# The second softmax exponential of 392 columns in three tiles of each image as a polynomial on VectorE, and a TensorE order planned with a look ahead

## What is computed

```python
g = clip(bn(conv1x1(l)), 0, 6)                       # values, 64 channels
theta = l[:, :32]
f = einsum('niab,nicd->nabcd', theta, theta)         # scores, 3136 x 3136 for each image
f = softmax(f.reshape(n, h * w, h, w), axis=1)       # over the queries
f = softmax(f.reshape(n, h * w, h * w), axis=2)      # over the keys
out = einsum('nabcd,nicd->niab', f, g)
out = bn(depthwise3x3(out / h * w))
return out + l
```

## Time and profile before

| | us |
|---|---|
| median of 3 runs | 5280.22 |
| lowest, highest | 5277.17, 5281.35 |
| the profiled execution | 5281.39 |
| its span, first to last instruction | 5279.5 |

### The profile page before, as it was taken

One profiled execution on the slowest core, in us unless ns is written; L12 is line 12 of the kernel. 1 busy time (PEld: TensorE's weight loads), 2 busy tenths in 40 slices (PEclk: granted clock), 3 DMA queues, 4 the chain that ended last, 5 costly groups with the idle time before them and its releaser, 6 DMA issues. The chain is left out here.

```text
span 5279.5 us, 89479 instructions
## 1 busy us (share of the span) xinstructions
PE 5199.9 (98%) x32626; PEld 2546.9 (48%) x32626; DVE 4437.3 (84%) x8974; ACT 5099.2 (97%) x3028; POOL 4447.5 (84%) x1857
## 2 busy tenths in 40 slices
PE   8999989999999999999999999999999999999997
PEld 3444444454445454545454444545454544454543
DVE  8888887888888888888888888888888888888887
ACT  7888889999999999999999999999999999999996
POOL 6666655898888998888999898899889899888897
PEclk9999989999999999999999999999999999999999
DMA  7888851222223222222221222232232322222221
GB/s 148 166 181 169 164 111 34 52 59 55 56 59 63 63 63 62 63 62 58 60 58 44 60 61 58 60 64 58 48 63 63 63 63 63 62 63 61 47 44 30
DMA packets 227138, 379.94 MB, mean 72 GB/s; under 512 B 158165, under 2 KB 175374, under 8 KB 216590
## 3 DMA queue, kind: packets, MB, share of 16 engines
q1 hardware_dynamic: 225520, 373.85, 33.9%
q10 hardware_dynamic: 1182, 0.37, 0.0%
HBM read 258.49 MB, written 102.74 MB: 68 GB/s over the span
## 5 line engine op out<-in xcount | busy, mean ns | idle before, releaser
L999 DVE TENSOR_SCALAR_CACHE_REDUCE at_ring<-at_S 128x1344 f32<-128x1344 f32 (+2 forms) x2352 | 2882.7, 1242 | 463.0 <-PE at_S L1122 446.4
L899 POOL TENSOR_TENSOR at_ZP<-at_ZP,at_ring 128x1568 f32<-128x1568 f32 x640 | 2280.2, 3605 | 151.0 <-ACT at_ring L948 140.9
L1153 PE MATMUL at_AV<-at_ring,at_GT 128*64 128x392 f32 x12800 | 2306.7, 501 | 7.2 <-issue 3.3
L942 ACT ACTIVATE at_ring<-at_ring,at_NM 128x3136 f32<-128x3136 f32 x784 | 2277.6, 2905 | 24.5 <-DVE at_NM L1008 23.0
L948 ACT ACTIVATE at_ring<-at_ring,at_RZ 128x3136 f32<-128x3136 f32 x784 | 2278.7, 2907 | 2.8 <-DVE at_RZ L1016 2.8
L1153 PEld LDWEIGHTS at_AV<-at_ring,at_GT 128*64 128x64 f32 x12800 | 856.2, 137 | 1153.5 <-issue 1113.8
L1122 PE MATMUL at_S<-at_THM,at_THS 128*128 128x448 f32 x5376 | 1386.1, 388 | 19.4 <-DVE at_ring L999 16.3
L1122 PEld LDWEIGHTS at_S<-at_THM,at_THS 128*128 128x128 f32 x5376 | 930.4, 189 | 643.2 <-DVE at_ring L999 299.6
L913 POOL TENSOR_TENSOR at_OUTB<-at_OUTB,at_ZB 128x1568 f32<-128x1568 f32 x248 | 885.6, 3571 | 16.9
L1159 PE MATMUL at_AV<-at_ring,at_ones 128*32 128x392 f32 x7168 | 676.8, 498 | 2.4 <-DVE at_ACC L1077 2.3
L518 DVE TENSOR_TENSOR l_U<-l_TY,l_XB 128x448 f32<-128x448 f32 x896 | 497.0, 617 | 90.6 <-PE l_TY L557 90.6
(11 more groups left out here) (78 smaller groups left out, 2475.7 us busy)
## 6 DMA issues: line engine op xcount, KB each, us to landing
at_THM<-hld SPq DMA_DIRECT2D x128, 392.0 KB, 6.5
at_THS<-hld SPq DMA_DIRECT2D x256, 192.0 KB, 4.1
l_X<-in_x SPq DMA_DIRECT2D x124, 392.0 KB, 7.4
at_CIN<-att SPq DMA_DIRECT2D x62, 406.0 KB, 7.7
at_ZB<-rzd SPq DMA_DIRECT2D x62, 406.0 KB, 7.7
yd<-l_YO SPq DMA_DIRECT2D x128, 196.0 KB, 5.0
att<-at_ACC SPq DMA_DIRECT2D x248, 98.0 KB
at_OUTB<-yd SPq DMA_DIRECT2D x62, 392.0 KB, 8.5
```

What stands on the lines that cost most here:

```text
L899: e.tensor_tensor(z, z, v, ALU.add).then_inc(g_add, 1)
L942: e.activation(v, v, ACT.Exp, bias=NM[:, i:i + 1], accum_out=ZS[:, i:i + 1]).then_inc(a_p1, 1)
L999: e.tensor_scalar(ring[:, s % RING, SC * a_:SC * b].rearrange("p (b w) -> p b w", w=SC), PS[:, k % 2, bank:bank + b - a_, 0:SC], 1.0, None ...
L1153: ins = e.matmul(dst[64 * j:64 * j + 64, 0:QC], GT[fl.n % 2][:, keys_of(fl.n, t), :], ring[:, slot, q:q + QC], start=(i == 0), stop=(i == ...
```

## The change

**In the program.** In the tiles 3, 11 and 18 of every image (`POLY_TILES`; 96 in all, none of them is one that two images share or that POOL adds up) ACT's second exponential leaves out the last 392 columns. DVE does these in six steps on SBUF, in place in the ring and with a scratch tile PT of 392 columns: a product of quadratic forms, scaled. The steps wait for each other by the semaphore v_p. PE's last part of the "o" and "z" fills of such a group waits for v_p also. To make room for PT, one buffer YT shrinks from 896 to 768 columns and bn1 moves into the memory that the first layer's tiles take and release.

**In the plan.** The steps are planned last of all that DVE could do, with 1.45 times the columns' time and 95 ns each; if POOL is busy, a step adds 400 ns to it. Where scores and a fill can both start, PE's choice is now found by going on with the plan both ways over 16 exponentials and taking the one with the lower "end of ACT less half of PE's fill work".

```diff
+PC = QC
+POLY_TILES = (3, 11, 18)
+PSTEPS = 6
+AHEAD = 16
+BACKLOG = 0.5
...
+    return [s for s in range(total) if len(tiles_of(s)) == 1 and tiles_of(s)[0][1] in POLY_TILES]
...
+        elif what == "p":
+            s, i = poly
+            end = t + 1.45 * PC / (1.92 if i in (0, PSTEPS - 1) else 0.96) + 95
+            if self.tg > t:
+                self.tg += 400
...
+    def worth(self, take):
+
+        run = self.ahead()
+        until = min(2 * self.work.total, self.n_a + AHEAD)
+        run.step(take=take)
+        while run.n_a < until and not run.over():
+            run.step()
+        return run.ta - BACKLOG * run.busy
+
+
+def plan(n_img):
+    p = Plan(Work(n_img))
+    while not p.over():
+        if not p.step(ask=True):
+            one, both, t_op, _ = p.choices()
+            scores, other = p.worth(True), p.worth(False)
+            p.step(take=(one if p.near() else both) <= t_op if abs(scores - other) < 1 else scores < other)
...
-        YT = [sb(f"YT{i}", [65, 896]) for i in range(2)]
+        YT = [sb("YT0", [65, 896]), sb("YT1", [65, 768])]
...
-        bn1 = sb("bn1", [65, 5, C])
...
+            bn1 = memory.enter_context(nc.sbuf_tensor("at_bn1", [65, 5, C], F32))
...
+        PT = sb("PT", [128, PC])
...
+                if h == 1 and s in poly:
+                    e.wait_ge(v_p, poly_steps(s))
...
-                v = ring[:, s % RING, :]
+                v = ring[:, s % RING, 0:HW - PC if s in poly else HW]
                 e.activation(v, v, ACT.Exp, scale=RZ[:, i:i + 1]).then_inc(a_p2, 1)
...
+            def poly_step(s, step):
+
+                v = ring[:, s % RING, HW - PC:HW]
+                before = poly_steps(s) - PSTEPS
+                if step == 0:
+                    e.wait_ge(v_r, s + 1)
+                    ins = e.tensor_scalar(v, v, RZ[:, s % 4:s % 4 + 1], POLY_SHIFT, ALU.mult, ALU.add)
+                elif step == 1:
+                    e.wait_ge(v_p, before + 1)
+                    ins = e.scalar_tensor_tensor(out=PT[:, :], in0=v, scalar=POLY_Z, in1=v, op0=ALU.add, op1=ALU.mult)
+                elif step == 2:
+                    ins = e.scalar_tensor_tensor(out=v, in0=v, scalar=POLY_T, in1=v, op0=ALU.add, op1=ALU.mult)
+                elif step == 3:
+                    e.wait_ge(v_p, before + 2)
+                    ins = e.scalar_tensor_tensor(out=PT[:, :], in0=PT[:, :], scalar=POLY_W, in1=PT[:, :],
+                                                 op0=ALU.add, op1=ALU.mult)
+                elif step == 4:
+                    e.wait_ge(v_p, before + 4)
+                    ins = e.scalar_tensor_tensor(out=v, in0=v, scalar=POLY_U, in1=PT[:, :], op0=ALU.add, op1=ALU.mult)
+                else:
+                    e.wait_ge(v_p, before + 5)
+                    ins = e.tensor_scalar(v, v, POLY_SCALE, POLY_END, ALU.mult, ALU.add)
+                ins.then_inc(v_p, 1)
...
+                        if fl.j == (1 if fl.kind == "z" else 3) and poly_steps(fl.first):
+                            e.wait_ge(v_p, poly_steps(fl.first))
```

More of the change, by code:

```diff
@@ L119, in __init__ @@
         self.units = [[(t, h) for h in range(width)] for t in tiles]
[L122 to L140, removed]
-    inf = float("inf")
[L142 to L164, removed]
-        else:
[L166 to L178, removed]
@@ new lines, in multiply @@
+    def multiply(self, t_s, t_op, f):
+        kind = "S" if t_s <= t_op else self.fills[self.cur].kind if self.cur is not None else f.kind
+        turn = 0 if self.COLS[kind] == self.mode else 200 if kind == "S" else 140
+        self.mode = self.COLS[kind]
+        if kind == "S":
+            self.tp = t_s + self.work.matmuls[self.n_s] + turn
+            self.end_s[self.n_s] = self.tp + 160
+            self.pe_order.append(("S", self.n_s, 0))
+            self.n_s += 1
+            return
+        if self.cur is None:
+            if kind == "g":
+                self.n_pre += 1
+            else:
+                self.n_main += 1
+            self.fills.append(f)
+            self.cur, self.at = len(self.fills) - 1, 0
+        f = self.fills[self.cur]
+        self.pe_order.append(("op", self.cur, self.at))
+        took = 224 if kind == "g" else 658
+        self.busy += took
+        self.tp = t_op + took + turn
+        self.t_fill[self.cur] = self.tp + 160
+        self.at += 1
+        if self.at == len(f.units):
+            self.ended[self.cur] = (3 * self.n_s - 1) // CT
+            if f.kind == "z" and f.j == 1:
+                self.group_end[f.n, f.i] = self.tp + 160
+            if f.kind == "z" and f.i == POOLED_IN:
+                self.summed[f.n, f.j] = self.tp + 160
+            self.cur = None
@@ new lines, in add_or_convolve @@
+    def add_or_convolve(self, t, what):
+        if what == "add":
+            n, t_, h = self.work.adds[self.n_add]
+            self.tg = self.end_add[n, t_, h] = t + (1700 if t_ == POOLED[0] else 3600)
+            self.pool_order.append(("add", (n, t_), h))
+            self.n_add += 1
+        else:
+            n, step = self.work.conv[self.n_conv]
+            self.tg = t + (3600 if step == 0 or step % 2 and step > 1 else 1620)
+            self.pool_order.append(("conv", n, step))
+            self.n_conv += 1
@@ L689, in build, with poly_steps @@
         block = ctx.enter_context(nc.Block())
+        def poly_steps(s):
+            return PSTEPS * sum(t <= s for t in poly)
         def added(n, t, h):
```

304 lines of the change are left out of this document (209 added, 95 removed).

## The result

| | us |
|---|---|
| median before, beside it | 5278.82 (5277.17 to 5281.35, 4 runs) |
| median after | 6224.68 (6200.23 to 6261.27, 4 runs) |
| ratio | 1.18, 95% interval 1.1761 to 1.184 |
| forecast | 6155, range 5480 to 6600 |

The account below looks back on a forecast made before the run. ACT was taken as the bound, with PE directly beside it. Each of 96 tiles loses 12.0 - 1.1 - 1.8 = 9.1 us, together 874, so 5281 + 874 = 6155 us, range 5480 to 6600.

Parts of the forecast that it names:

- The deciding term, the standstill: DVE's steps in the attention wait until GpSimd's instruction in progress ends: 11.7 us of waits a tile; chance 0.80.
- the one place that was priced: Tile 3 of image 10: the six steps wait 1.7, 3.6, 0, 1.8, 3.1 and 1.5 us behind GpSimd's adds, 11.7 together.
- The sum: Between a tile's first and last step 10.8 us becomes 22.8; less 1.1 and 1.8, 9.1 a tile, 874 in all.
- NM's lead: In the attention, NM is ready ahead of ACT's exponential, which takes up 1.1 us of a tile's added time.
- ACT's 33 us: Shorter second exponentials in 96 tiles save ACT 33 us, between 31 and 35; not taken off, since ACT waits.
- the rival without contention: DVE's steps in the attention meet no contention and the change works: 5248 us, between 5225 and 5275; chance 0.13.
- the prediction's PE rival: PE's spare 3 us in 1000 may not carry a shorter tile: 5265 instead of 5248; within another rival's 0.13.
- The order: PE's changed order holds the same matmuls: taken at nothing, 0 to -26 us kept for the range.
- Unhindered steps: Six DVE steps a tile, four of 0.62 and two of 0.36 us, less overlap: 2.7 us, 260 over 96 tiles.
- GpSimd's own delay: POOL's adds in the attention should show some 0.4 us more on a few hundred instructions.
- The clock: PE may lose its full clock when waiting, once in each stretch at some 3 us: 290 us on top, 6600.
- The sharing rival: DVE and GpSimd share, steps take about 1.45 times as long: 173 us, 5455, range 5290 to 5560; chance 0.07.

Follow-up runs that it names:

- pool_small: The changed kernel with every GpSimd instruction of the attention working on 8 columns, its sums and convolution mostly left out: 5257.36 us, ratio 0.996.
- one_input: The changed kernel with all six steps replaced by a tensor_scalar with one SBUF input and accumulator output, polynomial left out: 5260.85 us, ratio 0.9967.
- pool_writes_b: The changed kernel with GpSimd only writing: memsets in place of its sums and convolution, which are left out: 5291.52 us, ratio 1.0025.
- no_steps: The changed kernel without the six VectorE steps and their waits; ScalarE still leaves out the 392 columns: 5266.31 us, ratio 0.9979.
- order_alone: The changed kernel with no polynomial tile, keeping the look ahead order, smaller YT and all other edits: 5284.37 us, ratio 1.0011.

## Why the prediction was right

- **The deciding term, the standstill.** Predicted 13.7 us of steps for a tile (11.7 waiting, 2.0 own); measured 12.9 (10.5 until GpSimd's instruction ended, 2.4 own). At the one place that was priced, image 10's tile 3, GpSimd runs two adds and then four as before, and the six steps took 2.02, 3.82, 0.54, 2.61, 3.45 and 1.68 us: 14.1 in sum against 13.7, each within 0.4 us of its forecast wait and columns. Shown by pool_small (without GpSimd's columns: 3.0 us and no loss) and by one_input (without the property: 0.555 us each). That L1028 ended its own 0.83 us behind a GpSimd add was one long event, and it was enough: with GpSimd out of the way a step needs 0.42 and 0.22 us, where the forecast had 0.41 and 0.20. The forecast did not tell GpSimd's reads from its writes; pool_writes_b does, and it made no difference here, since the adds read.
- **The sum.** Its shape holds with the measured steps: 9.1 + 12.9 - 10.8 - 1.1 = 10.1 us a tile, against 9.85 from the medians and 9.7 from ACT's rate. The forecast had 9.1, one less, hence 6155 instead of 6225. Of that 1.0, 0.4 is the steps' own time (2.4 instead of 2.0, since 174 steps did not stand still and took 0.34 to 0.57 us), and 0.6 is that waiting fell by 1.2 us and not by the 1.8 I took off because GpSimd would be idle more often. GpSimd did thin out, from 894 to 759 us in 1000, and 402 of 576 steps stood still (0.70, where 0.89 less 15% gives 0.76); but each waited 2.5 us and not 2.2. Ten steps that sat through more than one GpSimd instruction (see the end) make 0.5 us a tile of it. In part errors cancel: from the first step's start to the last one's end a tile took 22.8 us in the changed kernel (12.9 of steps, 8.7 of other DVE work, 1.1 idle), 12.0 more than the 10.8 of before, and 2.1 of it was taken up, not the 1.1 of NM's lead. So the closeness of the total, within 70 us, is partly luck; the mechanism and the size of the waits are not.
- **ACT's 33 us counted at nothing.** Right for the slow kernel, since ACT waits. In the rival without contention I took 33 us in full and 5248; the runs without standstill came to 5257 to 5266. As far as the stretches tell, PE is the next bound and lets 13 to 22 us through. The 5265 of the prediction's PE rival is what no_steps shows.
- **The order.** Taken at nothing, between 0 and -26; order_alone shows +1 to +11 us by its interval, outside that range on the other side, if by little.
- **Unhindered steps.** scalar_tensor_tensor 0.56 us instead of 0.62, tensor_scalar 0.36 and 0.42 instead of 0.36: 3.0 us before the overlap is taken off, where I had 3.2.
- **GpSimd's own delay.** I expected 0.4 us more on a few hundred adds. Of the 640 L1073, the 263 in whose first 0.7 us a step ended have a median of 3.73 us, the others of 3.58: 0.15 us. So a held step's turn cost GpSimd less than the step's own time after it (0.22 or 0.42 us).
- **The clock.** It was to be a possible addition. The granted clock fell from 1.00 to 0.93 in the stretch, and PE needed 879.20 / 5128 = 171 ns a matmul instead of 161. The sum above closes without a term for it, so it was probably paid out of PE's waiting; no run separated it.
- **The sharing rival** (1.45 times) is refuted by the records: a scalar_tensor_tensor takes 0.54 to 0.57 us or ends behind a GpSimd instruction, there is no even stretch.

## What to carry over

Before work is moved to a VectorE with spare time, look at what GpSimd does at that moment: in these runs an instruction with two SBUF inputs waited for the end of GpSimd's reading instruction in progress, a tensor_scalar of the fast form with SBUF in and out for a writing one too, and every instruction queued behind it waited as well. In this ring of engines at 97 to 99%, the price was the length of GpSimd's instructions, not that of the step. Ask too what the next bound gives: here 33 us saved on ScalarE were worth 13 to 22 at best.
